# Splitting the down stage's ranks by token and turning them with an fp32r matmul

## The reference

```
hidden = x @ wi.T
       + 2 * (x @ common_wi_a.T) @ common_wi_b.T
       + 2 * (x @ Ai[e].T) @ Bi[e].T                 # e = expert of the sequence
hidden = relu(hidden)                                # 1024 features
out    = hidden @ wo.T
       + 2 * (hidden @ common_wo_a.T) @ common_wo_b.T
       + 2 * (hidden @ Ao[e].T) @ Bo[e].T
result = x + out
```

## Time and profile before

| what | value |
|---|---|
| device time, three executions | 133.82, 134.21 and 133.82 us, median 133.82 |
| span of the profiled execution | 132.4 us |
| its own device time | not listed apart; the median is 1.4 us above the span |
| PE busy | 125.6 us, 95% of the span, 826 matmuls |
| DVE busy | 58.4 us, 44% |
| ACT busy | 49.0 us, 37% |
| POOL busy | 15.0 us, 11% |
| granted TensorE clock | 1.000 (mean over the span) |
| chain that ended last, by engine | PE 88%, DVE 4%, DMA 3%, ACT 1%, issue 1%, SP's queue 1% |

### The profile page before, as it was taken

The page is one execution under the profiler, slowest core; times in us unless marked ns, Lnnn a source line. Parts: engine busy times, 40 slices in busy tenths (PEclk is TensorE's granted clock), DMA queues, the critical chain, the costliest instruction groups (busy, mean ns, idle before and its releaser), DMA issues.

```text
span 132.4 us, 2493 instructions
## 1 busy us (share of the span) xinstructions
PE 125.6 (95%) x826; PEld 115.2 (87%) x826; DVE 58.4 (44%) x102; ACT 49.0 (37%) x103; POOL 15.0 (11%) x47
## 2 busy tenths in 40 slices
PE   6999769999999999999999999999999999999981
PEld 6778569899999988889999988899999888899970
DVE  0174988676715364443062454450424544430232
ACT  4386828666342123333151323340413233321120
POOL 7031813004010120000010300000101000000000
PEclk9999999999999999999999999999999999999999
DMA  4759973020073522502201315004011200000112
GB/s 115 266 163 285 326 198 127 0 79 19 16 317 82 160 58 73 147 0 79 79 0 40 94 53 160 0 24 135 0 40 51 83 14 0 0 0 0 40 45 79
DMA packets 9994, 11.41 MB, mean 86 GB/s; under 512 B 2626, under 2 KB 7890, under 8 KB 9986
## 3 DMA queue, kind: packets, MB, share of 16 engines
q1 hardware_dynamic: 9010, 9.48, 24.2%
q10 hardware_dynamic: 976, 1.84, 3.7%
HBM read 7.90 MB, written 3.41 MB: 85 GB/s over the span
## 4 chain that ended last, share of the span: by engine, by line
PE 88%; DVE 4%; DMA 3%; ACT 1%; issue 1%; SPq 1%
PE bank_h L654 33%; PE bank_h L719 18%; PE bank_o L719 18%; PE bank_h L665 6%; DMA aic_nat<-in_L_cond_common_wi_a 3%; DVE bi_stack L524 3%; PE bank_x L614 2%; PE bank_x L635 2%; PE bank_x L623 2%; PE bank_o L614 2%; PE bank_h L728 2%; PE bank_o L736 1%; ACT bi_stack L440 1%; PE bank_h L736 1%; PE bank_h L614 1%
## 5 line engine op out<-in xcount | busy, mean ns | idle before, releaser
L654 PE MATMUL bank_h<-xT,wiT 128*128 128x512 f32 x192 | 49.8, 395 | 0.0
L654 PEld LDWEIGHTS bank_h<-xT,wiT 128*128 128x128 f32 x192 | 33.9, 189 | 5.7
L517 DVE SCALAR_TENSOR_TENSOR hid<-bank_h,hid 128x512 fp32r<-128x512 f32 x32 | 21.7, 689 | 23.8 <-ACT hid L458 23.8
L458 ACT ACTIVATE hid<-bank_h 128x512 fp32r<-128x512 f32 x32 | 18.8, 600 | 32.1 <-PE bank_h L665 32.1
L719 PE MATMUL bank_o<-wcat,hid 128*128 128x272 f32 x192 | 26.9, 293 | 0.0
L719 PE MATMUL bank_h<-wcat,hid 128*128 128x272 f32 x192 | 25.0, 289 | 0.0
L719 PEld LDWEIGHTS bank_o<-wcat,hid 128*128 128x128 f32 x192 | 24.6, 189 | 0.0
L719 PEld LDWEIGHTS bank_h<-wcat,hid 128*128 128x128 f32 x192 | 24.5, 188 | 0.0
L665 PEld LDWEIGHTS bank_h<-low_stack,bi_stack 128*128 128x128 f32 x64 | 11.3, 188 | 3.8 <-issue 1.7
L665 PE MATMUL bank_h<-low_stack,bi_stack 128*128 128x256 f32 x64 | 12.2, 283 | 1.5 <-DVE bi_stack L524 1.5
L517 DVE SCALAR_TENSOR_TENSOR lo_stack<-bank_h,lo_stack 16x128 fp32r<-16x128 f32 x16 | 4.5, 284 | 19.5 <-ACT lo_stack L468 19.3
(11 more groups left out here) (84 smaller groups left out, 102.1 us busy)
## 6 DMA issues: line engine op xcount, KB each, us to landing
out<-o_sb SPq DMA_DIRECT2D x16, 128.0 KB, 1.7
x_nat<-in_x SPq DMA_DIRECT2D x7, 256.0 KB, 2.8
bi_stack<-bi_parts SPq DMA_DIRECT2D x24, 64.0 KB, 2.3
wo_nat<-in_L_cond_wo SPq DMA_DIRECT2D x1, 1024.0 KB, 7.5
bi_parts<-biT ACTq DMA_DIRECT2D x2, 512.0 KB, 3.3
wi_nat<-in_L_cond_wi ACTq DMA_DIRECT2D x2, 256.0 KB, 4.0
wi_nat<-in_L_cond_wi SPq DMA_DIRECT2D x1, 512.0 KB, 4.4
ao_nat<-in_L_cond_experts_wo_a SPq DMA_DIRECT2D x1, 512.0 KB, 8.5
```

The costliest lines, as they stand in the source:

```text
L458: nc.scalar.activation(hid[HI][:, m, :], bank_h[m % 4][:, :], ACT.Relu).then_inc(hid_hi, 1)
L517: return nc.vector.scalar_tensor_tensor(out=out_, in0=src, scalar=0.0 if scale is None else scale, in1=hi.bitcast(F32), op0=op, op1=ALU.su ...
L654: nc.tensor.matmul(bank_h[m % 4][:, :], wiT[sw][:, k, f], xT[sx][:, k, :], start=(i == 0), stop=False)
```

## The change

The split into a high and a low part is moved ahead of the turn, to where the ranks lie by token. Step 1 now writes 6 instead of 8 copies of the ranks, as fp32r and with the factor ALPHA. The DVE then writes the low part into copy 2 of the six (`low_lo_part`, 128 partitions by 16 elements instead of 16 by 128), reading `out_bank[t]` instead of `tl_bank[t]`. The turn is a plain matmul of fp32r operands, `lo_sb` as the stationary one with 96 columns and a new fp32r identity `ident_r` as the moving one with 128. It waits for the DVE (`lo_split`) and for `ident_r`. ACT then copies the turned rows as they are, and `fin` waits for ACT (`tl_out`) instead of the DVE. POOL makes `ident_r` once, right behind `ident`.

```diff
@@ tiles and semaphores
+        ident_r = sb("ident_r", [P, P], F32R)
-        lo_sb = [sb(f"lo_sb{i}", [P, P // R, R]) for i in range(2)]
+        lo_sb = [sb(f"lo_sb{i}", [P, KP // R, R], F32R) for i in range(2)]
+        ident_r_ready = sem("ident_r_ready")
-        tl_done, tl_hi, tl_lo = sem("tl_done"), sem("tl_hi"), sem("tl_lo")
+        lo_split, tl_done, tl_out = sem("lo_split"), sem("tl_done"), sem("tl_out")
@@ POOL, behind the affine_select
+            pool.wait_ge(ident_ready, 1)
+            nc.gpsimd.tensor_copy(ident_r[:, :], ident[:, :]).then_inc(ident_r_ready, 1)
+            pool.wait_ge(ident_r_ready, 1)
+
@@ ACT, low_copy and tl_part
-                nc.scalar.copy(lo_sb[t % 2][:, :, :], ranks.unsqueeze(1).broadcast_to([P, P // R, R])).then_inc(lo_copied, 1)
+                nc.scalar.mul(lo_sb[t % 2][:, :, :], ranks.unsqueeze(1).broadcast_to([P, KP // R, R]), ALPHA).then_inc(lo_copied, 1)
-                nc.scalar.mul(lo_stack[t % 2][:, :], tl_bank[t][0:KP, 0:P], ALPHA).then_inc(tl_hi, 1)
+                nc.scalar.copy(lo_stack[t % 2][:, :], tl_bank[t][0:KP, 0:P]).then_inc(tl_out, 1)
@@ DVE
-            def tl_lo_part(step, t):
-                dve.wait_ge(tl_hi, step * TT + t + 1)
-                rows = lo_stack[t % 2][TL_LO:KL, :]
-                lo_part(rows, tl_bank[t][TL_LO:KL, 0:P], ALPHA, rows).then_inc(tl_lo, 1)
+            def low_lo_part(step, t):
+                dve.wait_ge(lo_copied, step * TT + t + 1)
+                at = RANK_AT[t // SEQ_TILES]
+                lo_part(lo_sb[t % 2][:, TL_LO // R, :], out_bank[t][:, at:at + R], ALPHA,
+                        lo_sb[t % 2][:, 0, :]).then_inc(lo_split, 1)
@@ DVE, down: low_lo_part(step, t) stands where tl_lo_part(step, t) stood, t = 0 to 3
@@ PE, turn_low and fin
-                pe.wait_ge(lo_copied, step * TT + t + 1)
+                pe.wait_ge(lo_split, step * TT + t + 1)
+                pe.wait_ge(ident_r_ready, 1)
-                nc.tensor.transpose(tl_bank[t][:, 0:P], lo_sb[t % 2][:, :, :].rearrange("p i r -> p (i r)"),
-                                    ident[:, :]).then_inc(tl_done, 1)
+                nc.tensor.matmul(tl_bank[t][0:KP, 0:P], lo_sb[t % 2][:, :, :].rearrange("p i r -> p (i r)"),
+                                 ident_r[:, :], start=True, stop=True).then_inc(tl_done, 1)
-                pe.wait_ge(tl_lo, step * TT + t + 1)
+                pe.wait_ge(tl_out, step * TT + t + 1)
```

More of the change, by code:

```diff
@@ L564, in down @@
             def down(step, more):
-                tl_lo_part(step, 0)
+                low_lo_part(step, 0)
                 if more:
@@ L568, in down @@
                 add(step, 0)
-                tl_lo_part(step, 1)
+                low_lo_part(step, 1)
                 add(step, 1)
-                tl_lo_part(step, 2)
+                low_lo_part(step, 2)
                 add(step, 2)
-                tl_lo_part(step, 3)
+                low_lo_part(step, 3)
                 if more:
```

## The result

| | before | changed |
|---|---|---|
| device time, median | 133.97 us (4 executions, 133.82 to 134.21) | 142.3 us (4 executions, 142.06 to 142.39) |
| span of the profiled execution | 132.4 us | 140.5 us |
| ratio of the times | | 1.0597, 95% interval 1.0565 to 1.063 |

The change costs 8.3 us. The forecast was 144.2 us with a range from 142.5 to 146.4, so sign and mechanism came out as forecast and the size did not: the span grew by 8.1 us, and I had reckoned with 10.4. (The profiled execution of the changed kernel took 142.25 us, 1.75 more than its span. Executions of the kernel before that were measured beside the experiments lie 1.8 above theirs in the median; my 1.4 compared a median with the span of another execution.)

The account below looks back on a forecast made before the run. The prediction took the kernel to be one stream of PE matmuls, busy 95% of the span. Stalls of 9.9 us plus 0.5 for the turns made 10.4, span 142.8, and with 1.4 around it 144.2 us; range 142.5 to 146.4.

Parts of the forecast that it names:

- The mechanism: Down stage, turns 1 to 3: PE waits for the DVE's add and subtraction after fin; 9.9 us over four steps.
- The subtraction's duration: New DVE subtraction of 16 elements per partition: 0.17 us, bounds 0.15 and 0.28.
- From one DVE operation to the next, already released, 0.04 us pass: DVE, from the add's end to the new subtraction's start: a gap of 0.04 us, counted in each stall.
- The turn itself: PE, 16 turns as fp32r matmuls: 0.14 us each instead of 0.11, +0.5 us; bounds -0.9 and +5.3.
- The sum: Whole kernel: stalls of 9.9 us plus 0.5 for the turns, 10.4 us more.
- The 1.4 us between span and time: Time around the profiled span, left at 1.4 us to go from a span of 142.8 to 144.2.
- Turn 0: First turn of each step, no add ahead of its subtraction: 0 us; up to 0.1 if step 0's 0.24 cover went.
- The last step, turn 3: End of the last step: turn 3 later by 0.49, the DVE's leg before fin 3 gone for -0.32; +0.17 us.
- PE works around the blocked turn: Rival: PE lets matmuls of main pass the waiting turn, leaving only +0.17 us, time 134.0; chance 0.04.
- Only a weight load is pulled ahead: Rival: PE loads the next operand during each of 11 stalls, saving 0.13 each, 1.4 us together: 142.8; chance 0.06.
- The turn is not one pass: Rival: the fp32r turns take the warm-up matmuls' slot, costing 5.3 instead of 0.5 us: 149.0; chance 0.06.
- The clock falls: Rival: PE's stalls drop its clock from 2.4 to 1.2 GHz, slowing main matmuls by +18 us, to 163; chance 0.03.

Follow-up runs that it names:

- e1_split_first: Changed kernel with the DVE's subtraction for tile t + 1 ahead of add t instead of behind it; 135.38 us, ratio 1.0087.
- e8_late_turn: Changed kernel with PE's turns 1 and 2 nine matmuls of main later and turn 3 behind all of low_in; 134.05 us, ratio 0.9998.
- e4: Kernel before with only the turn's form changed to an fp32r matmul, the ranks' low part lost; 134.78 us, ratio 1.0037.
- e2: Changed kernel with subtractions ahead of adds, tile 1's also ahead of x's, ACT's tile 1 copy earlier, turn 3 behind all low_in; 134.16 us, ratio 1.0013.
- e7: The kernel of e2 with the turn as an fp32 transpose of the split ranks; 134.1 us, ratio 1.0027.
- e9: The kernel of e2 measured again, against the kernel before; 134.37 us, ratio 1.0032.

## Why the prediction was wrong, point by point

- **The mechanism** (turn t waits for the subtraction, which stands behind add t - 1, which waits for fin t - 1): right. 12 waits, at the places named. e1_split_first and e8_late_turn each remove it, from the DVE's side and from PE's, and the loss goes with it.
- **The subtraction's duration**, 0.17 us from the line through two rows: right; 0.163 to 0.175 in the 16 instances. The gap of 0.06 from the DVE to PE held as well (41.46 to 41.52).
- **The failed step: "From one DVE operation to the next, already released, 0.04 us pass".** It was measured on a pair of operations with different start partitions and applied to a pair with the same. The distance from the add's start to the turn's load was to be 0.42 + 0.04 + 0.17 + 0.06 = 0.69; it is 0.56 at all three turns of step 0 (41.52 - 40.96, 45.60 - 45.04, 48.17 - 47.61). 12 x 0.13 = 1.6 us too much. I treated this gap as known and gave it no lower bound. The trace of the kernel before held the warning, in its round 2: two subtractions of `x`, with a mean of 684 ns by their group, take 1.29 us together and so overlap by 0.08.

```profile
67.16 1.29 DVE L531 TENSOR_TENSOR xT<-bank_x,xT 128x512 fp32r<-128x512 f32 x2 [0.47 <-ACT xT L450]
L531 DVE TENSOR_TENSOR xT<-bank_x,xT 128x512 fp32r<-128x512 f32 x8 | 5.1, 684 | 1.4 <-ACT xT L450 1.4
```

- **The turn itself**, +0.5 us: wrong in sign, by the traces. Where PE does not wait, the slots of fin and turn together did not change (e4). After a stall the turn gives some of it back: from turn 1's load to fin 1's it is 3.08 us (41.52 to 44.60) where it was 3.11 before (40.53 to 43.64), so about 8 x -0.03 = -0.2. Together 0.7 too much.
- **The sum:** 10.4 - 1.6 - 0.7 = 8.1 us, the measured growth of the span; up to the last fin it is 8.0, so 0.1 at most is left over.
- **The 1.4 us between span and time** were too low: it is 1.75 in the profiled execution. So the forecast missed the span by 2.3 us and the time by 1.9 only; the other 0.4 of the miss was hidden by this error, which was luck.
- **Turn 0** at no cost: right to within 0.1 in the changed kernel. Its load came at 38.00 instead of 37.92, held back by ACT's late copy (37.49 instead of 37.14). But the forecast took the copy's start as fixed and gave the loss of the cover 0.1 at most. In e8_late_turn round 1 lost 0.37 there, in e1_split_first 0.5.
- **The last step, turn 3:** forecast +0.49 - 0.32. The wait grew by 0.36 and the end shrank by 0.36 (from the turn's load to fin's it is 0.65, it was 1.01), so 0.
- **The rivals.** *PE works around the blocked turn*: out, the 24 loads of `main` start behind the turn at every stall. *Only a weight load is pulled ahead*: out in this form, since no load of `main` starts ahead of the turn's; the nearest thing is that it may start with it or 0.08 behind it instead of 0.11. *The turn is not one pass*: out, by its slot of 0.13 in e4. *The clock falls*: out, as the granted clock of the changed kernel was 1.00 up to the last matmul, which ends at 137.9, and lower only behind it. The last stretches, with their length and then busy time of PE, PEld, DVE, ACT and POOL, clock, and DMA:

```profile
133.00:136.00 3.00, 2.40 (x20) 2.19 (x18) 0.51 (x2) 0.26 (x1) 0.00 (x0) 1.00 0.13 44
136.00:138.00 2.00, 0.91 (x4) 0.36 (x3) 0.61 (x3) 0.51 (x2) 0.00 (x0) 1.00 0.19 65
138.00:140.50 2.50, 0.00 (x0) 0.00 (x0) 0.32 (x1) 0.00 (x0) 0.00 (x0) 0.67 0.16 53
```

- **The range** missed by 0.2 us. Its lower end took in a cheaper turn, but no gap of the DVE under 0.04. It was also not the sum of its own parts: the cheaper turn and the pulled-ahead loads, 1.4 us each, would have reached 141.4 together, and I wrote "hardly lower together" without a reason.

What stays open: why the time outside the span is longer in e2, e7 and e9 (1.9 to 2.2 us in the median, against 1.8). Their spans are equal to those of the kernel before within 0.2 us, their times 0.1 to 0.3% above. No version of the study beats the kernel before.

## What to carry to other kernels

When an operation moves from behind a handover to ahead of it, look at what stands before it in its own engine's queue and who that waits for: here an add that waited for PE stood between two operations of PE, and 12 such loops cost 8 us, although the operation itself became shorter (0.17 us instead of 0.28). Such a loop is cut from either side, by putting the awaited operation ahead of the unrelated one, or by giving the waiting engine enough independent work ahead of the wait. And the gap between two operations of an engine is a number of that pair: take it from a pair whose start partitions match in the same way.

## What the hardware showed that I had not expected

- The add and the subtraction on DVE overlapped by 0.08 us where both start at partition 0, and kept a gap of 0.04 where they start at different ones. That made 1.5 us between two kernels with the same work. In e2_all_early, with the subtraction ahead of the add, the add starts 0.09 behind a subtraction of 0.17:

```profile
73.40 0.17 DVE L523 SCALAR_TENSOR_TENSOR lo_sb<-bank_o,lo_sb 128x16 fp32r<-128x16 f32 x1 [1.47 <-ACT lo_sb L470]
73.49 0.41 DVE L568 TENSOR_TENSOR o_sb<-bank_o,x_res 128x256 f32<-128x256 f32 x1
```

- An fp32r matmul with 128 moving and 96 stationary columns took a slot of 0.12 to 0.13 us in a busy PE, no more than those with 256 or 272 moving columns (0.12 to 0.14), and an fp32 transpose of 128 columns 0.11.
- After a stall of about 1 us PE starts the load of the following matmul 0.08 us (fp32r) or 0.00 us (fp32 transpose) behind that of the first one, instead of 0.11.
